# Cross-attention and mixture-of-experts kernel: value tiles, gate and ranks moved to the end of TensorE's turn

## Chip, cores and metric

The kernel runs on one core of a Trainium2 chip, in one launch. The metric is the device time of an execution in microseconds (us). A measured difference of about 0.3% is what can be told from none.

## The reference

One layer on x [16, 256, 512] with a context [16, 256, 256]. It is float32; the mask is all true.

```python
x = x + xattn(layernorm(x), ctx, mask, Wq, Wk, Wv, Wo)
x = x + ffn(layernorm(x), ...)
# xattn: 16 heads of 128, 8 key/value heads (two query heads share one)
scores = q @ k.T / sqrt(128); attn = softmax(scores); out = (attn @ v) @ Wo
# ffn: sigmoid gate over 32 experts, in 4 groups of 8; the 2 best groups, then the 4 best experts
# slot = how many earlier tokens (of all 4096) chose the same expert; those past CAP are dropped
h = silu(buf @ w1[e]) * (buf @ w3[e]); y = h @ w2[e]        # 32 experts, 512 -> 256 -> 512
out = sum_k weight_k * y_k + (silu(x @ sg) * (x @ su)) @ sd  # plus a shared expert, 512 wide
```

Since slots count tokens in order, the ranks (how many earlier tokens chose the same expert) are accumulated batch after batch.

## The kernel before

**Numbers.** Every float32 product is made from float16 halves: a value is split into a high half (`.hi`, written by ScalarE) and a low half (`.lo`, the rest, by VectorE or GpSimdE), and `products` issues three matmuls, high x high, high x low, low x high (lines 1777 to 1779). So each PSUM result that is used further is read twice: ScalarE's `..._high`, then VectorE's `..._low`.

**Turns.** The main part is a loop of 128 turns (`TURNS`), i = 8 b + j: batch b (16), key/value head j (8). Four compute engines and SyncE (SP, which issues most DMAs) each have their own program, written out by hand and in order; they meet only at semaphores. In turn i TensorE does:
- `scores(i)`: 12 matmuls of 256 columns, into ps_score0 and ps_score1
- `filler(fill(b, j))`: one extra job into the bank ps_fill1: a value tile (6 matmuls of 512 columns; four per batch, for the batch after, in turns 1, 3, 4, 6; in the first two batches in other turns), or in turn 5 the gate of the batch before (24 small ones)
- `query(i + 1)`: 24 matmuls of 256 columns; `key(i + 1)`: 6, into ps_fill1 as well
- `attend(i - 1)`: 6 matmuls of 512 columns, into ps_score1; its left operand are the probabilities turned by DMA
- `project(i - 2)`: 21 matmuls of 256 columns into ps_out0, ps_out1, ps_head and ps_fill0, where they add up over the 8 turns of a batch
- in turn 7 the ranks of the batch before (5 small ones), into ps_fill1.

The jobs that share ps_fill1 have one order, the list `held`; each waits (`emptied`) until the one before it has been read: keys by `key_low`, value tiles by `value_low` (VectorE, line 1352), the gate by `gate_exp_neg` (ScalarE), ranks by `place` (VectorE).

**The other engines in turn i.** VectorE: `maxima(i)` (line 1411, four, from ps_score), the batch's own work for that turn, the filler's `value_low`, `prob_scales` (lines 1418 and 1420, after ScalarE's exponentials), `query_low(i + 1)` (1346), two `probs_low` (1436), `key_low(i + 1)` (1341), `last_high` (1427), two more `probs_low`, then more of the batch's work. ScalarE: `sums_high(i - 2)` (1083), exponentials (1061) with the filler's `value_high` (984) between the second and the third, `query_high` (977), two `probs_high` (1069), `key_high` (971), the third, then `head_copy(i - 1)` (1076), which reads what attend wrote. GpSimdE: `sums_low(i - 2)` (786: one operation of 896 columns), the work of the batch, then `sums(i - 1)` (778, 779, 781), sums and differences of the copied head output. The projection is a product of 2 x 2 blocks with 7 products instead of 8, and these sums are its operands; `project` waits for `sum_lo`.

**Work of a batch, by turn j.** VectorE: turn 0 `place`, `pick(position)`, `find_slots` of b - 2, and at its end `pick(score)`, `choose_9` to `choose_11` (the weights); turn 1 at its end `residual_first`; turn 2 `residual_rest` (1308 to 1316), at its end the statistics of x1 (1263, 1268); turn 3 at its end the statistics of x of the next batch; turn 4 `xn2_rest` (1362); turn 5 `xn_rest` (1357), at its end `choose_0`, `choose_1`; turn 6 `choose_2` to `choose_4`, at its end `choose_5`, `choose_6`; turn 7 `choose_7`, `choose_8`, and `ctx_low`. GpSimdE: turn 3 `inv_std` of x1 (726, 729) and `x1_norm` (748, two tiles), turn 4 `inv_std` of x and `x_norm` (738, two tiles), turns 1, 2, 5, 6 a quarter each of `record` (831, indirect DMAs that write the table of slots). ScalarE and SP follow: `xn2_high` in turn 3, `xn_high` in turn 4, `turn_xn2` in turn 4, `turn_xn` in turn 6.

In the first batch the weights are split too (`weight_high`, `weight_low`, and `combine` on GpSimdE for Wo).

**After the loop.** The shared expert runs in `piece`s: up pieces (two products, tanh, product) and down pieces, which ScalarE copies to `shared_y`, from where `add_shared` adds them to the output by an accumulating DMA (815). ScalarE's copy of group n waits until the additions of group n - 2 have landed; those of groups 1 and 2 are counted together. Then come the 32 experts with gathered rows.

## Time and profile before

| | us |
|---|---|
| median of three runs | 1707.92 |
| lowest, highest | 1705.89, 1711.77 |
| profiled execution, its own time | 1704.77 |
| its span, first to last instruction | 1703.0 |
| matmuls busy | 1585.2 (93%) |
| VectorE busy | 1380.7 (81%) |
| ScalarE busy | 1053.2 (62%) |
| GpSimdE busy | 1035.9 (61%) |
| mean granted clock of TensorE | 0.987 |

PE is TensorE's matmul side, PEld its weight loads, DVE VectorE, ACT ScalarE, POOL GpSimdE. Matmuls are pipelined: one of 256 columns lasts 0.27 us and the next starts 0.11 us after it, so distances between starts count, not durations. A row of windows gives the stretch from:to, its length, the busy time and count of PE, PEld, DVE, ACT and POOL, the granted clock, the DMA engines' busy share and GB/s. A row `L1352 ... out<-in` names the line, the tile written and those read; "arena" is a tile that holds weights, values and probabilities, h_both the head output, weight_in[1] the halves of its sums. A clock of 1.00 is 2.4 GHz. The loop begins at 17.97 us; batch 10, whose turns are shown below, from 805.76 to 881.27.

### The profile page before, as it was taken

Reading aid. Unit: us, or ns where it says so; the run is one execution under the profiler, and the core shown is the slowest. Engines: PE = TensorE matmul, PEld = TensorE weight load, DVE = VectorE, ACT = ScalarE, POOL = GpSimd, SP = SyncE. Lnnn points to the kernel's source line nnn. Section 1 sums busy time; section 2 is a strip of 40 time slices with the busy share of each in tenths; the row PEclk is TensorE's granted clock in tenths of the full one; section 3 lists DMA queues with packets and bytes.
Section 4 is the critical chain, followed back from the end, with each engine's and each line's share of the span. In section 5 each row is a group of like instructions: output and inputs, shape, how many; then the busy total and the mean of one; then the engine's idle time right before and its main releaser. Section 6 shows DMA issues by size and latency. Waiting matters only on the chain. (4 is left out here: it accounts for less than half of the span.)

```text
span 1703.0 us, 36611 instructions
## 1 busy us (share of the span) xinstructions
PE 1585.2 (93%) x12583; PEld 1186.1 (70%) x12583; DVE 1380.7 (81%) x3723; ACT 1053.2 (62%) x2487; POOL 1035.9 (61%) x1004
## 2 busy tenths in 40 slices
PE   7778999999999999999999999999999899999995
PEld 4556767777777777777777777777776666666662
DVE  7788989998998989899988999898777156766763
ACT  5666676766666666666667666666644156666663
POOL 2766585857667586767768586776766533434332
PEclk9899999999999999999999999999999999999998
DMA  7545774636455454545555454544765558988843
GB/s 208 142 89 110 151 170 101 125 61 134 91 104 104 92 119 76 132 87 117 96 100 107 88 119 77 130 89 100 149 187 198 149 175 228 253 239 237 243 75 50
DMA packets 403751, 225.72 MB, mean 133 GB/s; under 512 B 348769, under 2 KB 360033, under 8 KB 403185
## 3 DMA queue, kind: packets, MB, share of 16 engines
q1 hardware_dynamic: 387104, 197.05, 48.5%
q0 software_dynamic: 15904, 25.29, 8.6%
q8 instruction: 103, 1.69, 0.4%
q10 hardware_dynamic: 560, 1.05, 0.2%
q14 instruction: 80, 0.65, 0.1%
HBM read 95.54 MB, written 44.47 MB: 82 GB/s over the span
## 5 line engine op out<-in xcount | busy, mean ns | idle before, releaser
L786 POOL TENSOR_TENSOR weight_in<-h_both,weight_in 128x896 f16<-128x896 f32 x128 | 244.0, 1907 | 97.5 <-ACT weight_in L1083 97.5
L1777 PE MATMUL ps_query<-xn_both,arena 128*128 128x256 f16 x1056 | 288.7, 273 | 1.0 <-DMA xn_both<-xn_half 1.0
L1778 PE MATMUL ps_query<-xn_both,arena 128*128 128x256 f16 x1056 | 288.6, 273 | 0.0
L1779 PE MATMUL ps_query<-xn_both,arena 128*128 128x256 f16 x1056 | 288.5, 273 | 0.0
L1083 ACT ACTIVATE weight_in<-h_both 128x896 f16<-128x896 f32 x128 | 121.6, 950 | 260.1 <-POOL h_both L781 256.2
L1436 DVE SCALAR_TENSOR_TENSOR arena<-arena,prob_scale 128x256 f16<-128x256 f32 x512 | 270.8, 569 | 0.6 <-ACT arena L1069 0.6
L1061 ACT ACTIVATE arena<-arena,neg_max 128x256 f32<-128x256 f32 x512 | 253.0, 495 | 25.4 <-DVE neg_max L1411 25.2
L778 POOL TENSOR_TENSOR h_both<-h_both 128x256 f32<-128x256 f32 x128 | 112.4, 878 | 194.8 <-ACT h_both L1076 194.6
L1069 ACT ACTIVATE arena<-arena,prob_scale 128x256 f16<-128x256 f32 x384 | 179.5, 499 | 71.8 <-DVE prob_scale L1420 69.9
L1411 DVE CUSTOM_DVE_ANT_0 arena<-ps_score,mask_add 128x256 f32<-128x256 f32 x512 | 185.6, 418 | 42.4 <-PE ps_score L1779 41.4
L831 POOL DMA_INDIRECT slot_table<-entry,slot_at x128 | 135.9, 1062 | 45.7 <-issue 31.1
L1777 PE MATMUL ps_out<-arena,weight_in 128*128 128x256 f16 x512 | 141.4, 276 | 13.4 <-POOL weight_in L786 13.4
L1777 PE MATMUL ps_score<-k_both,q_t 128*128 128x256 f16 x512 | 139.6, 273 | 8.6 <-issue 8.4
L1779 PE MATMUL ps_out<-arena,weight_in 128*128 128x256 f16 x512 | 141.4, 276 | 0.0
L1778 PE MATMUL ps_out<-arena,weight_in 128*128 128x256 f16 x512 | 141.4, 276 | 0.0
L1779 PE MATMUL ps_score<-k_both,q_t 128*128 128x256 f16 x512 | 139.7, 273 | 0.0
L1778 PE MATMUL ps_score<-k_both,q_t 128*128 128x256 f16 x512 | 139.7, 273 | 0.0
L1777 PE MATMUL ps_fill<-ctx_both,arena 128*128 128x256 f16 x256 | 69.8, 273 | 56.2 <-DVE arena L1352 54.4
L1777 PEld LDWEIGHTS ps_query<-xn_both,arena 128*128 128x128 f16 x1056 | 103.5, 98 | 20.5 <-DMA xn_both<-xn_half 1.5
L1553 DVE SCALAR_TENSOR_TENSOR arena<-arena 128x1024 f16<-128x1024 f32 x96 | 116.8, 1225 | 1.0 <-ACT arena L1095 1.0
L1778 PEld LDWEIGHTS ps_query<-xn_both,arena 128*128 128x128 f16 x1056 | 103.5, 98 | 18.9
L1779 PEld LDWEIGHTS ps_query<-xn_both,arena 128*128 128x128 f16 x1056 | 103.5, 98 | 12.3
(339 smaller groups left out, 4831.0 us busy)
## 6 DMA issues: line engine op xcount, KB each, us to landing
arena<-w SPq DMA_DIRECT2D x96, 512.0 KB, 6.1
out_rows_dram<-weight_in POOLq DMA_DIRECT2D x32, 256.0 KB, 4.7
x_in<-x SPq DMA_DIRECT2D x15, 512.0 KB, 4.9
out_rows_dram<-x SPq DMA_DIRECT2D x30, 256.0 KB, 4.7
xn_rows<-xn_half SPq DMA_DIRECT2D x15, 512.0 KB
x2t_kept<-xn_both SPq DMA_DIRECT2D x13, 512.0 KB, 3.0
ctx_in<-ctx_t SPq DMA_DIRECT2D x16, 256.0 KB, 3.5
arena<-arena SPq DMA_TRANSPOSE x256, 3.1
```

The lines of the kernel that those rows point to most:

```text
L778: pool.tensor_tensor(o_full[:, 4:6, :], o_full[:, 0:2, :], o_full[:, 2:4, :], ALU.add).then_inc(*own.up())
L786: pool.tensor_tensor(l_t.lo, o_full[:, :, :], l_t.hi, ALU.subtract).then_inc(sum_lo, 1)
L831: pool.indirect_dma_start(slot_table, bass.IndirectOffsetOnAxis(ap=slot_at[z % 2][:, t, k:k + 1], axis=0), entry[z % 2][:, t, k, :], None, ...
L1061: act.activation(probs[:, c, :], probs[:, c, :], ACT.Exp, bias=neg_max[:, c:c + 1], scale=-1.0, accum_out=prob_sum[:, c:c + 1]).then_inc(e ...
L1069: act.activation(p_rows[:, c, 0, :], probs[:, c, :], ACT.Copy, scale=prob_scale[:, c:c + 1]).then_inc(norm_hi, 1)
L1083: act.activation(l_t.hi, o_full[:, :, :], ACT.Copy, scale=1.0).then_inc(sum_hi, 1)
L1411: dve.tensor_tensor_reduce(out=probs[:, c, :], in0=ps_score[h][:, t * S:(t + 1) * S], in1=mask_add[b % 2][:, :], scale=-SCORE_SCALE, scala ...
L1436: dve.scalar_tensor_tensor(p_rows[:, c, 1, :], probs[:, c, :], prob_scale[:, c:c + 1], p_rows[:, c, 0, :], ALU.mult, ALU.subtract).then_in ...
L1553: dve.scalar_tensor_tensor(expert_w[e % HELD].lo[:, at], expert_in[e % AHEAD][:, at], W_S, expert_w[e % HELD].hi[:, at], ALU.mult, ALU.sub ...
L1777: pe.matmul(dst, a.hi, b.hi, start=start and n == 0, stop=False, skip_group_check=shared)
L1778: pe.matmul(dst, a.hi, b.lo, start=False, stop=False, skip_group_check=shared)
L1779: m = pe.matmul(dst, a.lo, b.hi, start=False, stop=stop and n == len(pairs) - 1, skip_group_check=shared)
```

## The change

The extra job in ps_fill1 moves behind `project` in TensorE's turn. It is emptied in the next turn: by ScalarE first thing, by VectorE after the maxima. The ranks of batch b - 2 become such a job, in turn 0 (place, pick(position) and find_slots in turn 1). `head_copy` moves ahead of ScalarE's third `probs_high`. `sums_low` becomes three operations of 256, 256 and 384 columns, and `sum_lo` counts three per turn. `x_norm` moves from GpSimdE to VectorE (turn 4), where `x_norm` was already defined for the first batch; `x1_norm` does one tile in turn 3 and one in turn 4. The high and low halves of xn2 and xn and their turning and storing move a turn later. Of the routing, `choose_0` and `choose_1` move from the end of turn 5 to that of 6, `choose_2` to `choose_4` from turn 6 to 7, `choose_5` and `choose_6` from the end of 6 to that of 7, `choose_7` and `choose_8` from 7 to the next turn 0, `pick(score)` to `choose_11` from the end of turn 0 to that of 3. After the loop, the second `add_shared` and two `late_split` come earlier in GpSimdE's order, and the pieces 0 and 1 and the last routing steps move.

```diff
@@ order of the jobs
+            if b > 1 and j == 0:
+                return ("rank", b - 2)
...
+            held += [("key", i + 1)] if i + 1 < TURNS else []
             held += [fill(b, j)] if fill(b, j) else []
-            held += [("key", i + 1)] if i + 1 < TURNS else []
-            held += [rank_of(b, j)] if rank_of(b, j) else []
+        held += [("rank", B - 2)]
@@ SP: turn_xn2 and store_xn2 from turn 4 to 5, keep_x2t from 6 to 7
-                if j == 4 and b:
+                if j == 5 and b:
                     for t in range(TB):
                         turn_xn2(b - 1, t)
@@ GpSimdE
             def sums_low(i):
                 pool.wait_ge(sum_hi, i + 1)
-                pool.tensor_tensor(l_t.lo, o_full[:, :, :], l_t.hi, ALU.subtract).then_inc(sum_lo, 1)
+                for at in (slice(0, 2), slice(2, 4), slice(4, LEFT)):
+                    pool.tensor_tensor(l_t.lo[:, at, :], o_full[:, at, :], l_t.hi[:, at, :], ALU.subtract).then_inc(sum_lo, 1)
...
-                if 1 <= i <= KV:
-                    combine(i - 1)
...
-                if j == 3 and b:
-                    x1_norm(z)
-                if j == 4 and a < B:
-                    x_norm(a)
-                if j in (1, 2, 5, 6) and b > 1:
-                    record(b - 2, (1, 2, 5, 6).index(j))
+                if j in (3, 4) and b:
+                    x1_norm(z, j - 3)
+                if j in (5, 6, 7) and b > 1:
+                    record(b - 2, j - 5)
+                if j == 0 and b > 2:
+                    record(b - 3, 3)
...
+                if i < KV:
+                    combine(i)
...
             add_shared(0)
+            add_shared(1)
             for part in range(RECORDS):
                 record(z, part)
...
-            add_shared(1)
+            for k in (20, 21):
+                late_split(k)
             pool.wait_ge(in_table, 16)
@@ ScalarE
+                if i:
+                    filler(fill(*divmod(i - 1, KV)))
                 if i >= 2:
                     sums_high(i - 2)
                 exps(i, range(0, TB))
...
-                filler(fill(b, j))
                 exps(i, range(TB, CELLS))
...
                 if i + 1 < TURNS:
                     key_high(i + 1)
-                probs_high(i, range(TB, CELLS - 1))
                 if i:
                     head_copy(i - 1)
-                if j == 3 and b:
+                probs_high(i, range(TB, CELLS - 1))
+                if j == 4 and b:
                     for t in range(TB):
                         xn2_high(b - 1, t)
-                if j == 4 and b + 1 < B:
+                if j == 5 and b + 1 < B:
                     for t in range(TB):
                         xn_high(b + 1, t)
@@ VectorE
                 maxima(i)
+                if i:
+                    filler(fill(*divmod(i - 1, KV)))
...
-                if j == 0 and b > 1:
+                if j == 1 and b > 1:
                     place(b - 2)
                     dve.wait_ge(placed, b - 1)
                     pick(position)
                     find_slots(b - 2)
                 if j == 2 and routed:
                     residual_rest(z)
-                if j == 4 and routed:
-                    for t in range(TB):
-                        xn2_rest(z, t)
-                if j == 5 and a < B:
+                if j == 4 and a < B:
+                    x_norm(a)
+                if j == 6 and a < B:
                     for t in range(TB):
                         xn_rest(a, t)
-                if j == 6 and routed:
+                if j == 7 and routed:
                     choose_2()
                     choose_3()
                     choose_4()
-                if j == 7 and routed:
+                if j == 0 and b > 1:
                     choose_7()
-                    choose_8(z)
-                filler(fill(b, j))
+                    choose_8(b - 2)
                 prob_scales(i)
...
@@ TensorE
                 scores(i)
-                filler(fill(b, j))
                 if i + 1 < TURNS:
                     for h in range(PAIR):
                         query(i + 1, h)
...
-                if i == TURNS - 1:
-                    piece(1)
                 if i >= 2:
                     project(i - 2)
-                filler(rank_of(b, j))
+                filler(fill(b, j))
```

## Rows read from the trace of the kernel before

**Rows 1.** Windows: one batch's turns 0, 2 to 7; twelve batches; two batches.
```profile
805.76:814.45 8.69, 8.45 (x75) 6.60 (x72) 8.45 (x24) 5.31 (x15) 4.11 (x4) 1.00 0.44 63
...
825.28:833.45 8.17, 8.17 (x71) 6.76 (x69) 7.83 (x22) 5.68 (x15) 5.28 (x7) 1.00 0.40 46
833.45:843.28 9.83, 9.63 (x77) 7.26 (x75) 8.65 (x26) 6.71 (x18) 9.21 (x9) 1.00 0.75 179
843.28:853.69 10.41, 9.63 (x78) 7.27 (x75) 9.08 (x24) 7.90 (x19) 10.16 (x10) 1.00 0.81 130
853.69:862.46 8.77, 8.77 (x95) 7.34 (x93) 7.71 (x19) 5.68 (x16) 6.30 (x7) 1.00 0.42 110
862.46:872.97 10.51, 9.63 (x77) 7.27 (x75) 10.04 (x44) 6.37 (x16) 6.44 (x7) 1.00 0.58 111
872.97:881.27 8.30, 8.30 (x76) 6.88 (x74) 7.17 (x21) 5.57 (x15) 3.85 (x5) 1.00 0.58 104
276.77:1183.32 906.55, 865.80 (x7266) 679.93 (x7264) 818.35 (x2438) 595.01 (x1548) 638.41 (x612) 1.00 0.50 102
...
117.93:276.77 158.84, 145.81 (x1218) 113.82 (x1216) 144.45 (x410) 108.04 (x275) 102.86 (x97) 1.00 0.65 137
```

**Rows 2.** Waits, 276.77 to 1183.32 us: who for whom, total, times, longest.
```profile
PE ps_fill L1777 <- DVE arena L1352: 36.2, 47, 1.2
```

**Rows 3.** Timeline of TensorE, turn 6: start, duration, instruction, [idle before].
```profile
863.77 0.38 PE L1777 MATMUL ps_fill<-arena,ctx_both 128*128 128x512 f16 x1
...
865.07 0.27 PE L1777 MATMUL ps_query<-xn_both,arena 128*128 128x256 f16 x1
...
867.58 0.27 PE L1779 MATMUL ps_query<-xn_both,arena 128*128 128x256 f16 x1
868.73 0.27 PE L1777 MATMUL ps_fill<-ctx_both,arena 128*128 128x256 f16 x1 [0.88 <-DVE arena L1352]
```

**Rows 4.** Timeline of VectorE, turns 2 and 3 of the batch.
```profile
826.69 0.41 DVE L1411 CUSTOM_DVE_ANT_0 arena<-ps_score,mask_add 128x256 f32<-128x256 f32 x1
...
828.06 0.69 DVE L1308 SCALAR_TENSOR_TENSOR x<-ps_out,x 128x512 f32<-128x512 f32 x1
...
830.71 0.17 DVE L1418 RECIPROCAL prob_inv<-prob_sum 128x4 f32<-128x4 f32 x1
...
832.85 0.34 DVE L1427 TENSOR_SCALAR arena<-arena,prob_scale 128x256 f16<-128x256 f32 x1
...
834.38 1.27 DVE L1263 BATCH_NORM_STATS2 stats<-x 128x6 f32<-128x512 f32 x2
...
835.85 0.41 DVE L1411 CUSTOM_DVE_ANT_0 arena<-ps_score,mask_add 128x256 f32<-128x256 f32 x1
...
839.12 0.18 DVE L1418 RECIPROCAL prob_inv<-prob_sum 128x4 f32<-128x4 f32 x1 [0.23 <-ACT arena L1061]
```

**Rows 5.** Timeline of VectorE, turns 0 and 1 of the batch.
```profile
815.79 0.74 DVE L1515 TENSOR_TENSOR picked<-one_hot,score 128x128 f32<-128x128 f32 x2
...
817.98 0.42 DVE L1411 CUSTOM_DVE_ANT_0 arena<-ps_score,mask_add 128x256 f32<-128x256 f32 x1
```

**Rows 6.** Timeline of GpSimdE, turns 3 and 4 of the batch.
```profile
843.09 0.73 POOL L778 TENSOR_TENSOR h_both<-h_both 128x256 f32<-128x256 f32 x1
...
846.09 2.00 POOL L786 TENSOR_TENSOR weight_in<-h_both,weight_in 128x896 f16<-128x896 f32 x1
```

**Rows 7.** The page's groups: busy time, mean ns, idle before.
```profile
L786 POOL TENSOR_TENSOR weight_in<-h_both,weight_in 128x896 f16<-128x896 f32 x128 | 244.0, 1907 | 97.5 <-ACT weight_in L1083 97.5
```

**Rows 8.** Timeline of VectorE, turn 4 of the batch.
```profile
845.66 2.98 DVE L1362 SCALAR_TENSOR_TENSOR xn_half<-weight_in,xn_half 128x512 f16<-128x512 f32 x2
```

**Rows 9.** One line's instructions on VectorE: shortest, median, longest ns.
```profile
L1284 DVE TENSOR_SCALAR x<-x_in,mean_var,rstd x2: 529/738/948, 6.5 to 7.4; 128x512 f32<-128x512 f32 x2
```

**Rows 10.** Timeline of ScalarE, turn 4 of the first batch.
```profile
81.28 0.63 ACT L991 ACTIVATE xn_half<-x 128x512 f16<-128x512 f32 x1 [1.44 <-POOL x L738]
```

**Rows 11.** Timeline of ScalarE after the last turn.
```profile
1340.93 0.60 ACT L1042 ACTIVATE weight_in<-ps_query 128x512 f32<-128x512 f32 x1 [10.35 <-DMA out_rows_dram<-weight_in]
```

More of the change, by code:

```diff
@@ L425, in fill @@
             return None
-        def rank_of(b, j):
-            return ("rank", b - 1) if j == KV - 1 and b else None
         before = {}
@@ L1054, in filler @@
                     value_high(ps_fill[1], *at)
-                else:
+                elif kind == "gate":
                     gate_exp_neg(*at)
@@ L1646, in dve_program @@
                     query_low(i + 1)
+                else:
+                    piece(0)
                 probs_low(i, range(0, TB))
@@ L1654, in dve_program @@
                     ctx_low(1)
-                if i == TURNS - 1:
-                    piece(0)
-                if j == 0 and b > 1:
-                    pick(score)
-                    choose_9()
-                    choose_10()
-                    choose_11(b - 2)
                 if j == 1 and routed:
@@ L1666, in dve_program @@
                         x1_stats_row(z, t)
+                if j == 3 and b > 1:
+                    pick(score)
+                    choose_9()
+                    choose_10()
+                    choose_11(b - 2)
                 if j == 3 and a < B:
@@ L1669, in dve_program @@
                         x_stats_row(a, t)
-                if j == 5 and routed:
+                if j == 4 and routed:
+                    for t in range(TB):
+                        xn2_rest(z, t)
+                if j == 6 and routed:
                     choose_0(z)
                     choose_1()
-                if j == 6 and routed:
+                if j == 7 and routed:
                     choose_5()
```

56 lines of the change are left out of this document (26 added, 30 removed).

## The prediction

> **What bounds the kernel now.** I read the windows of one steady batch first, turn by turn, then who waits for whom, then the timelines of TensorE, VectorE and GpSimdE around the waits. Batches 3 to 14 take 906.55 us together, 75.55 each, at full granted clock [rows 1]. A turn without extra work is 8.17 us of TensorE (turn 2 of a batch, no idle time); the gate matmuls add 0.60 (turn 5: 8.77), the ranks 0.13 (turn 7: 8.30) [rows 1], and a value tile 1.30 (its first matmul to the first of the query) [rows 3]. With four value tiles a batch is 8 x 8.17 + 4 x 1.30 + 0.60 + 0.13 = 71.3 us of TensorE. So 4.25 us per batch are waits: 0.5 in turn 0, 0.36 in turn 3, 0.94 in turn 4, 1.04 in turn 6, and by difference 1.4 in turn 1 [rows 1].
>
> Nearly all of it has one cause. The key matmuls write the PSUM bank that the value tile of the same turn has just filled, and VectorE's value_low empties that bank only behind the maxima: 47 waits, 36.2 us as the view counts idle time [rows 2]. In turn 6 the queries' last matmul starts 1.15 us before the key's first (867.58, 868.73), where 0.11 is the normal distance [rows 3]. TensorE is the bound, then, and VectorE holds it for about 1 us in the value turns. But VectorE is no idle helper: 818.35 of the 906.55 us are busy [rows 1].
>
> **The change, part by part.**
>
> *Value tile, gate, ranks at the end of the turn.* TensorE's work is the same. The tile is now read by ScalarE first thing in the next turn, during the scores, and by VectorE after its maxima; the next key comes 12 + 24 matmuls of 0.109 us (12 scores take 1.31 [rows 1, 3]) = 3.93 us after the turn's start. Maxima can start about 1.0 us in (an estimate: half of the scores, 0.65, and the 0.27 that a matmul takes [rows 3]); they take 1.37 (826.69 to 828.06) and value_low about 0.7, as other steps of its size from PSUM do [rows 4]. It ends at 3.1: the wait of 4.25 per batch goes wherever VectorE comes to its maxima on time, with 0.8 us to spare. Queued behind value_low is residual_rest in turn 2, x_norm in turn 4, choose_2 to 4 in turn 7, and then prob_scales, for which ScalarE waits.
>
> *Where VectorE is not on time.* The parts of VectorE per turn, by start-to-start times. Turn 2: maxima from 1.0 to 2.4, value_low to 3.1 (new here), residual_rest 2.65 (828.06 to 830.71) to 5.7, prob_scales up to the end of key_low 2.14 (830.71 to 832.85, where the next step starts) to 7.9. That is inside 8.17, by 0.3. The rest of the probabilities takes 1.53 (832.85 to 834.38), the statistics 1.47 (834.38 to 835.85) [rows 4]: VectorE ends at 10.9, which is 2.7 into turn 3. Before, it was 2.4 into it (835.85 against 833.45) [rows 1, 4].
> Turn 3: maxima start to reciprocal took 3.27 (835.85 to 839.12) with ScalarE's value copy in between [rows 4]; without its 0.6 (estimate from the 0.7 of its VectorE twin) 2.7. So reciprocal at 5.4, key_low done at 7.5, probabilities at 9.1, and 0.3 more because the head copy now stands before ScalarE's third probabilities: 9.4. Now the moved weights of the routing, pick(score) to choose_11: 2.19 (815.79 to 817.98) [rows 5], plus 0.5 for a collision (below): 12.1. The statistics of x, 1.47: 13.6. Turn 3 is 9.47 long, so VectorE is 4.1 into turn 4, less what turn 3 itself waits.
> Turn 3's own wait: GpSimdE's inv_std now as before waits for the statistics (2.7), takes about 1 us (in turn 4 the sums start at 843.09 with 0.73, 2.0 in all by estimate, and the low halves at 846.09 [rows 6]), and the low halves follow in 2.4: 6.2. TensorE's projection needs them at 8.17 - 21 x 0.109 = 5.88; before, the tile stood in between. Wait 0.35.
> Turn 4: maxima from 3.8 to 5.1, value_low to 5.9, key possible at 3.93: wait 1.95. Behind it x_norm (1.5), then probabilities; key_low ends before 9.6 and TensorE needs it at 8.17 + 1.95 = 10.1. Turn 5 has almost nothing for VectorE, and it catches up. Turns 6, 7, 0, 1 I find without a wait: the long steps end after 7 to 8 us against the 8.17.
> Waits after: 0.35 + 1.95 = 2.3 per batch instead of 4.25. Saving 1.95, twelve batches: **23.4 us**.
> Bounds: if VectorE loses no time to collisions and the weights overlap better, 1.3 are left (saving 35); if it loses another 2 us between turn 2 and turn 4, 4.3 are left (saving 0).
>
> *Three short low-half operations instead of one.* One operation of 896 columns is 1.9 us on average [rows 7] and 2.00 here; 256 columns take 0.73 [rows 6]. From these two the fixed part is about 0.25, so three cost 0.73 + 0.73 + 0.96 = 2.4: half a microsecond more on GpSimdE and later for the projection. In turn 4 the single operation ended 4.8 after the turn's start (848.09 against 843.28) with inv_std's 1.0 ahead of it; elsewhere that makes 3.8, with the half 4.3, against 5.88: a margin of 1.6. If each part also waits for one two-input step of VectorE of 0.69, three cost 4.5, and the margin is gone. What they give: VectorE's pair of xn2_rest took 2.98 us (845.66) where a step of this size takes 0.69 [rows 4, 8]; 1.7 were lost until GpSimdE's 2.00 us operation ended at 848.09 [rows 6]. With short ones a loss is at most about 1. The Trainium skill, "SBUF — State Buffer", section "Who interferes with whom", gives the rule: the read port that the two share is held for a whole instruction and the other engine blocks fully, when VectorE has two SBUF inputs or a two-port mode; the trace agrees here (1.7 us). By the same rule x_norm, moved to VectorE, can be blocked too, which speaks against that part; its two tiles would be 1.9 instead of 1.5 and the sum 0.4 per batch worse at most, and only if key_low were then late, which it is not.
>
> *x_norm from GpSimdE to VectorE, x1_norm in two turns.* VectorE takes 0.74 per tile, 0.53 to 0.95 [rows 9]: 1.5 in turn 4, behind value_low, hidden under the wait counted above; GpSimdE is rid of both tiles. Halving x1_norm lets the sums of turn 3 go first. The turned and stored xn rows move a turn later on SP, past one turn_probs, but queries need them only in the next batch's first turn; I cost them at nothing. Cover: about 4 us, and a miss would stand in turn 7.
>
> *Head copy sooner, routing later.* The copy comes when the attend matmuls end, so at most 0.5 us sooner: nothing by itself. The choose steps moved from turn 7 to 0 and the slots from 0 to 1 take the load from the turn that ran 8.45 busy of 8.69 [rows 1]; counted above. Records move with them, on a GpSimdE that has room.
>
> *Start and end.* In turn 4 of the first batch ScalarE waits twice some 1.5 us for GpSimdE's x_norm (81.28) and the weights of the next turns queue behind it [rows 10]. That goes, but the loads of wo bound the turns after it: **4 us**, between 0 and 8. Batches 1 and 2 take 158.84 for 72.6 + 71.3 of work, 15 us of waits [rows 1]; the same cause, one value tile more: **7 us**, between 3 and 11. At the end ScalarE waits 10.35 us for an accumulating DMA (1340.93) [rows 11]. The second such transfer is issued sooner, but ScalarE waits for the third as well, and that one stays behind the gathers with two more splits ahead of it: no gain there; about **1 us** from earlier attention in the last turn.
>
> **Sum.** 23.4 + 4 + 7 + 1 = 35 us. The profiled execution took 1704.77 (span 1703.0), so 1669.5; the median of the runs shown is 3.15 above it: 1672.5, said as 1672.
>
> **Rivals.**
> 1. *No waits left.* VectorE is on time everywhere, as in turn 6: 12 x 4.25 = 51, start 8, batches 1 and 2 11, end 1: 71 us, 1637. Against it: turns 2 to 4 carry 2.19 more than before in turn 3 and 0.7 more in turn 2.
> 2. *The wait only moves.* The key waits for value_low as long in turn 4 as in all turns now: 0 from the steady batches and 8 to 12 from the rest: 1697. For it: every microsecond of lateness between turn 2 and turn 4 is a microsecond of TensorE, twelve times, and GpSimdE now puts six blocking operations where there were four.
> 3. *Slower: the projection waits for the low halves in every turn.* It comes 1.3 us sooner in four turns, its operand 0.5 to 2.6 later. If the three parts end 0.8 after TensorE is ready, that is 8 x 0.8 = 6.4 per batch against 4.25, and 12 x 2.15 = 26 us: 1734. It decides from 0.53 us per turn. Against it: the margin of 1.6.
>
> **How the numbers follow.** My forecast 0.62 (own range 1656 to 1688), rival 1 0.13, rival 2 0.16, rival 3 0.07, something else slower 0.02. A measurement of this kernel tells about 0.3% (5 us) from no change. Rival 2 gives half of its chance to a gain over that and half to none; so faster 0.83, same 0.08, slower 0.09. The range takes in rival 2 and most of the way to rival 1: 1648 to 1697.
>
> **What would show it.** TensorE's waits on ps_fill from L1352's successor gone in turns 1, 3 and 6, and left in turn 4, near 2 us; steady batches near 73.6 us; VectorE's maxima of turn 4 3 to 4 us after the scores' start; three GpSimdE operations of 0.7 to 1.0 us; no DVE pair near 3 us. I am wrong if ps_out waits for GpSimdE in several turns of a batch, if a batch is under 72 us, or if the key waits in turns 1, 3 or 6.

## The result and the profile after

The changed kernel takes 1712.39 us (median of 20 runs, 1706.55 to 1716.11), the kernel before, run beside it, 1707.81. The ratio is 1.0023, 95% interval 1.0014 to 1.0032: slower by 0.23%, some 4 us, where 35 us were forecast as a gain. The profiled executions took 1711.89 and 1704.77 us, with spans of 1710.2 and 1703.0.

The windows of a usual steady batch (number 13, turns 0 to 7), turn 4 of batch 10, then batches 3 to 14, batches 1 and 2 and the first batch. After the length stand the busy times (and counts) of TensorE's matmuls and weight loads, VectorE, ScalarE and GpSimdE, the granted clock, the DMA share and GB/s.

```profile
1037.47:1046.12 8.65, 8.46 (x76) 6.79 (x74) 8.34 (x29) 5.57 (x15) 6.35 (x8) 1.00 0.47 121
1046.12:1056.06 9.94, 9.64 (x82) 7.19 (x80) 9.57 (x27) 5.46 (x15) 5.66 (x9) 1.00 0.42 79
1056.06:1064.54 8.48, 8.33 (x70) 6.67 (x69) 8.34 (x23) 6.12 (x16) 2.84 (x6) 1.00 0.21 41
1064.54:1074.53 9.99, 9.80 (x75) 7.17 (x76) 8.76 (x25) 5.71 (x16) 8.77 (x12) 1.00 0.69 175
1074.53:1086.15 11.62, 9.63 (x77) 7.28 (x76) 11.29 (x33) 7.18 (x18) 7.60 (x10) 1.00 0.46 65
1086.15:1095.12 8.97, 8.94 (x94) 7.27 (x93) 8.07 (x21) 7.31 (x18) 6.74 (x10) 1.00 0.75 120
1095.12:1104.59 9.47, 9.47 (x83) 7.33 (x79) 8.36 (x22) 5.80 (x16) 7.71 (x9) 1.00 0.84 181
1104.59:1112.76 8.17, 8.17 (x71) 6.75 (x70) 7.86 (x34) 6.26 (x16) 5.66 (x8) 1.00 0.19 36
...
847.46:860.75 13.29, 11.30 (x76) 7.96 (x75) 12.96 (x35) 7.18 (x18) 8.38 (x10) 0.87 0.44 70
...
282.36:1187.56 905.20, 870.89 (x7263) 679.77 (x7260) 844.81 (x2461) 592.37 (x1548) 617.44 (x780) 1.00 0.51 102
126.75:282.36 155.61, 147.09 (x1213) 114.12 (x1212) 143.74 (x401) 108.48 (x275) 97.70 (x122) 0.99 0.62 135
17.74:126.75 109.01, 79.03 (x540) 56.81 (x541) 82.57 (x174) 66.48 (x148) 58.75 (x72) 0.87 0.49 128
```

A steady batch takes 75.43 us (905.20 / 12), before 75.55 [rows 1]; 73.6 was forecast. Turns 6 and 7 have no wait left, and turn 4 waits 11.62 - 9.47 = 2.15, close to the forecast 1.95. Against the forecast turn by turn the excess is 0.35, 0.47, 0.31, 0.17, 0.20, 0.20, 0 and 0, or 1.7 per batch. The average of the twelve is 0.14 above this batch. In two of them, 3 and 10, turn 4 takes 13.3 us: the granted clock is 0.87 there, because it fell to half (the 1.2 GHz level) for 3.4 us, within 1.4 us of the end of the key's wait of 1.99. The matmuls are busy 11.30 instead of 9.63, so this costs 1.7 us each time, 0.28 per batch on average; in the other ten, eight of them with the same wait, the clock stayed at 1.00.

By stretches the 7.2 us of span are: first batch 99.96 to 109.01 (+9.05, forecast -4), batches 1 and 2 -3.23 (forecast -7), steady batches -1.35 (forecast -23.4), turns 0 to 7 of the last batch up to the last scores +0.86, the end +2.10 (forecast for both together -1), and -0.23 ahead of the first turn. These are one profiled execution of each kernel, and a few microseconds of such a difference are its scatter (see below the table).

The largest waits of TensorE's matmuls in batches 3 to 14 of the changed kernel (who for whom, total, times, longest):

```profile
PE ps_fill L1776 <- DVE arena L1346: 22.7, 12, 2.0
PE ps_score L1776 <- DMA arena<-arena: 7.2, 14, 1.5
PE ps_score L1776 <- DVE neg_max L1405: 1.3, 7, 0.2
```

The key's wait for value_low was met 47 times before [rows 2]; it is met 12 times now, once per batch, in turn 4. The two rows of ps_score are the heads' matmuls (attend): 8.5 us. They are not quite new: in the kernel before they waited twice, 1.0 us in all. They write the bank that the scores filled, so they wait for the maxima of their own turn, and they read the turned probabilities of the turn before. The forecast followed the key, the projection and the scores, and never these. By the distances between the matmuls' starts they now wait 0.29, 0.44 and 0.36 us in turns 0, 1 and 3; the 0.2 in turn 5 stands before the key, as in turn 4. TensorE's timeline in turns 0, 1 and 4 of batch 13 (start, duration, instruction, [idle before]):

```profile
1042.41 0.38 PE L1776 MATMUL ps_score<-arena 128*128 128x512 f16 x1 [0.19 <-DVE neg_max L1405]
...
1051.18 0.38 PE L1776 MATMUL ps_score<-arena 128*128 128x512 f16 x1 [0.30 <-DMA arena<-arena]
...
1080.61 0.27 PE L1776 MATMUL ps_fill<-ctx_both,arena 128*128 128x256 f16 x1 [1.99 <-DVE arena L1346]
```

And VectorE from turn 3 into turn 4:

```profile
1067.56 0.41 DVE L1405 CUSTOM_DVE_ANT_0 arena<-ps_score,mask_add 128x256 f32<-128x256 f32 x1
...
1074.48 1.01 DVE L1509 TENSOR_TENSOR picked<-one_hot,score 128x128 f32<-128x128 f32 x2
...
1076.79 0.17 DVE L1530 TENSOR_TENSOR entry<-weight,weight_inv 128x8 f32<-128x8 f32 x1
1076.87 1.28 DVE L1257 BATCH_NORM_STATS2 stats<-x_in 128x6 f32<-128x512 f32 x2
...
1078.35 0.41 DVE L1405 CUSTOM_DVE_ANT_0 arena<-ps_score,mask_add 128x256 f32<-128x256 f32 x1
...
1079.72 0.75 DVE L1346 SCALAR_TENSOR_TENSOR arena<-ps_fill,value_scale,arena 128x512 f16<-128x512 f32 x1
```

The maxima of turn 4 start 3.82 us into the turn (1078.35 - 1074.53; forecast 3.8), behind weights of 2.39 (1076.87 - 1074.48) and statistics of 1.5. So the mechanism of turn 4 is as forecast. What was not forecast shows in the groups of VectorE over the twelve batches, the low halves and the last high half of the probabilities, before and after (mean ns behind the busy time):

```profile
L1436 DVE SCALAR_TENSOR_TENSOR arena<-arena,prob_scale 128x256 f16<-128x256 f32 x386 | 197.3, 552 | 0.0
L1427 DVE TENSOR_SCALAR arena<-arena,prob_scale 128x256 f16<-128x256 f32 x96 | 35.3, 368 | 0.0
```
```profile
L1430 DVE SCALAR_TENSOR_TENSOR arena<-arena,prob_scale 128x256 f16<-128x256 f32 x385 | 234.6, 649 | 4.8 <-issue 3.1 <-ACT arena L1062 0.8
L1421 DVE TENSOR_SCALAR arena<-arena,prob_scale 128x256 f16<-128x256 f32 x96 | 44.6, 465 | 0.0
```

The same instructions take longer: (234.6 - 197.3 + 44.6 - 35.3) / 12 = 3.9 us more of VectorE per batch in these two groups.

### The profile page after: what moved, and what is told of

The parts are those of the page before. It is cut to its first block and busy times, and to the rows that moved or that the text cites. A ratio compares the mean times of both kernels' runs of the same rounds, so it can differ in the third digit from the quotient of the medians.

```text
span 1710.2 us, 36852 instructions
## 1 busy us (share of the span) xinstructions
PE 1593.9 (93%) x12583; PEld 1187.5 (69%) x12583; DVE 1411.9 (83%) x3753; ACT 1050.2 (61%) x2487; POOL 1010.9 (59%) x1230
## 5 line engine op out<-in xcount | busy, mean ns | idle before, releaser
L778 POOL TENSOR_TENSOR weight_in<-h_both,weight_in 128x256 f16<-128x256 f32 (+1 forms) x384 | 299.4, 807 | 123.8 <-ACT weight_in L1076 114.7
L1430 DVE SCALAR_TENSOR_TENSOR arena<-arena,prob_scale 128x256 f16<-128x256 f32 x512 | 312.4, 650 | 18.7 <-ACT arena L1062 14.5
L769 POOL TENSOR_TENSOR h_both<-h_both 128x256 f32<-128x256 f32 x128 | 101.5, 793 | 139.8 <-ACT h_both L1069 139.5
L1776 PE MATMUL ps_score<-arena 128*128 128x512 f16 x256 | 98.1, 383 | 16.4 <-DMA arena<-arena 11.0
L1777 PEld LDWEIGHTS ps_query<-xn_both,arena 128*128 128x128 f16 x1056 | 103.5, 98 | 12.2
L1778 PEld LDWEIGHTS ps_query<-xn_both,arena 128*128 128x128 f16 x1056 | 103.5, 98 | 12.1
```

Source lines behind the costliest of these rows:

```text
L769: pool.tensor_tensor(o_full[:, 4:6, :], o_full[:, 0:2, :], o_full[:, 2:4, :], ALU.add).then_inc(*own.up())
L778: pool.tensor_tensor(l_t.lo[:, at, :], o_full[:, at, :], l_t.hi[:, at, :], ALU.subtract).then_inc(sum_lo, 1)
L1430: dve.scalar_tensor_tensor(p_rows[:, c, 1, :], probs[:, c, :], prob_scale[:, c:c + 1], p_rows[:, c, 0, :], ALU.mult, ALU.subtract).then_in ...
L1776: pe.matmul(dst, a.hi, b.hi, start=start and n == 0, stop=False, skip_group_check=shared)
L1777: pe.matmul(dst, a.hi, b.lo, start=False, stop=False, skip_group_check=shared)
L1778: m = pe.matmul(dst, a.lo, b.hi, start=False, stop=stop and n == len(pairs) - 1, skip_group_check=shared)
```

## The experiments

In this table all spans are of profiles. "Steady" is batches 3 to 14 divided by 12; "end" is from the last turn's scores to the end. "Profiled" is the time of the execution that the spans are from. Stretches come from the starts of the scores' first matmuls; the ratio is to the kernel before, run beside it.

```
kernel                          median   ratio (95%)              profiled  first   steady  end
before                          1707.8                           1704.8    99.96   75.55  458.6
after                           1712.4   1.0023 (1.0014-1.0032)  1711.9   109.01   75.43  460.7
late_head                       1687.7   0.9882 (0.9865-0.9899)  1689.1   104.20   74.19  462.7
early_head                      1757.3   1.0290 (1.0271-1.0308)  1750.7   105.19   78.00  457.4
one_low                         1719.7   1.0075 (1.0056-1.0094)  1712.2   107.27   75.43  461.5
tiles_alone                     1706.5   0.9995 (0.9983-1.0006)  1704.3   101.89   75.15  457.2
fill_move                       1681.8   0.9849 (0.9828-0.9870)  1679.0   101.15   74.00  456.7
copy_soon_sums_wait             1695.4   0.9925 (0.9905-0.9945)  1695.4   109.19   74.12  462.0
one_low_late_head               1682.0   0.9845 (0.9825-0.9865)  1683.6   105.88   73.80  460.8
norm_end_late_head              1678.4   0.9822 (0.9803-0.9840)  1676.4   102.06   73.43  462.6
sums_after_lows                 1693.9   0.9912 (0.9898-0.9926)  1695.1   106.07   74.36  462.4
weights_t5                      1680.6   0.9835 (0.9819-0.9851)  1680.8   111.41   72.81  464.0
weights_t5_late_head            1666.7   0.9760 (0.9740-0.9780)  1666.4   104.17   72.55  463.0
w5_late_head_norm_end           1664.6   0.9741 (0.9725-0.9757)  1665.4   103.27   72.53  463.0
w5_late_head_one_low_norm_end   1669.0   0.9774 (0.9760-0.9789)  1668.6    98.86   73.09  463.5
fill_move_w5                    1716.6   1.0052 (1.0038-1.0066)  1713.4   101.23   75.90  464.1
slots_after_residual            1691.3   0.9900 (0.9885-0.9914)  1691.3   105.56   74.18  464.4
```

Kernels whose first batch is the same program show how far single profiles scatter: 109.01 (after) and 111.41 (weights_t5); 104.20, 104.17 and 105.56 (late_head, weights_t5_late_head, slots_after_residual); 102.06 and 103.27 (the two with x_norm behind the probabilities and three low halves). The clock's share of it shows in the granted clock of the first batch, 0.86 to 0.92 in these.

### The place of the head copy

late_head undoes it in the changed kernel:

```
-                if i:
-                    head_copy(i - 1)
                 probs_high(i, range(TB, CELLS - 1))
+                if i:
+                    head_copy(i - 1)
```

> The changed kernel with one part undone: ScalarE copies the heads after its third probabilities again, as before the change. Theory (start): in turn 2 of the first batch the sooner copy waits for GpSimdE's low halves behind a weight combination, ScalarE's third probabilities wait behind it, the load of x queues behind the turned probabilities and the next weights behind that; so the first batch falls from 109.0 us back to about 100, steady batches stay at 75.4, and the time is about 1703, ratio to the kernel before 0.997. Rival (the place of the copy costs nothing, the first batch is late because of the tiles or because the combinations stand elsewhere): within 1.5 us of the changed kernel, 1712.

early_head makes the opposite edit in the kernel before.

> The kernel before with one part of the change alone: the head copy in front of ScalarE's third probabilities. Theory (start): the first batch gets 5 to 9 us longer (99.96 us before), the rest stays, so 1713 to 1717, ratio 1.003 to 1.005. Rival (costs nothing): ratio within 0.001 of 1.

1687.7, 24.7 us under the changed kernel and far more than the 9 expected: the first batch gives 4.8, batches 1 and 2 give 2.9, and a steady batch 1.24 (14.9 in all), which the theory had called unchanged. Of these 1.24, 0.28 are the two falls of the clock, which late_head doesn't have in batches 3 to 14. By the matmuls' starts the heads' waits fall from 1.1 to 0.5 per batch, and the key's in turn 4 from 2.05 to 1.64.

In the kernel before, the edit costs 50 us where 5 to 9 were expected, 2.45 in each steady batch. Some 1.4 of the 2.45 are clock: in ten of the twelve batches the granted clock of turn 1 is 0.87 or 0.88, and the turn takes 13.3 to 14.1 us, where it takes 11.8 and 12.1 in the two others and 10.8 in the kernel before. In each of the ten the clock fell after a wait of 2.0 to 2.8 us. By the trace the wait comes from VectorE, which is late because its low halves wait for ScalarE's third probabilities, 37.7 us in the twelve steady batches. Turn 1 of batch 10, and that group:

```profile
845.63:859.53 13.90, 11.30 (x77) 7.79 (x75) 10.41 (x28) 6.33 (x16) 7.06 (x10) 0.88 0.28 54
```
```profile
L1436 DVE SCALAR_TENSOR_TENSOR arena<-arena,prob_scale 128x256 f16<-128x256 f32 x384 | 211.7, 591 | 39.9 <-ACT arena L1069 37.7
```

In the changed kernel that wait is small (0.8). What the copy does there can be read in turn 2. Changed kernel, ScalarE, GpSimdE and VectorE:

```profile
1063.70 0.59 ACT L1069 ACTIVATE h_both<-ps_score 128x512 f32<-128x512 f32 x1
1064.18 0.50 ACT L1062 ACTIVATE arena<-arena,prob_scale 128x256 f16<-128x256 f32 x1
```
```profile
1064.37 0.91 POOL L769 TENSOR_TENSOR h_both<-h_both 128x256 f32<-128x256 f32 x1 [3.84 <-ACT h_both L1069]
1065.24 0.64 POOL L770 TENSOR_TENSOR h_both<-h_both 128x128 f32<-128x128 f32 x1
```
```profile
1064.72 1.45 DVE L1430 SCALAR_TENSOR_TENSOR arena<-arena,prob_scale 128x256 f16<-128x256 f32 x2
```

late_head, GpSimdE and VectorE in the same turn of batch 10:

```profile
820.29 0.91 POOL L769 TENSOR_TENSOR h_both<-h_both 128x256 f32<-128x256 f32 x1 [3.50 <-ACT h_both L1069]
```
```profile
820.14 1.34 DVE L1430 SCALAR_TENSOR_TENSOR arena<-arena,prob_scale 128x256 f16<-128x256 f32 x2
```

With the sooner copy GpSimdE's sums have begun when VectorE comes to its pair of low halves, and both halves of the pair meet them (0.85 and 0.68 us one by one); with the late copy the first half starts ahead of the sums (0.48 and 0.95). In this turn that is only 0.1 us. Over the twelve batches the low halves fall from 649 to 614 ns on average, and the last high half, which meets the sums in turns 0, 1 and 7, from 465 to 354:

```profile
L1430 DVE SCALAR_TENSOR_TENSOR arena<-arena,prob_scale 128x256 f16<-128x256 f32 x386 | 221.5, 614 | 0.0
L1421 DVE TENSOR_SCALAR arena<-arena,prob_scale 128x256 f16<-128x256 f32 x96 | 34.0, 354 | 0.0
```

Together that is 2.0 us of VectorE per batch, and its maxima of turn 4 start 3.3 us into the turn instead of 3.7. The next run tells that from ScalarE's order. It keeps the copy where the change has it and holds the sums back until the third probabilities are made:

```
                 pool.wait_ge(head_copied, i + 1)
+                if i + 1 < TURNS:
+                    pool.wait_ge(norm_hi, (CELLS - 1) * (i + 2))
```

> The changed kernel, head copy where it has it, with one more wait: GpSimdE's sums of the heads start only when ScalarE has made the third probabilities of the turn, which is when they start in late_head. Theory (steady batches: not ScalarE's order costs, but the sums that start 0.5 us sooner and stand in the way of VectorE's low half of the third probabilities, 0.85 instead of 0.48 us): steady batches 74.2 plus or minus 0.3 as in late_head; the first batch stays at 109, since there ScalarE's probabilities themselves wait behind the copy; time 1694 to 1700. Rival (ScalarE's third probabilities 0.5 us later are the cost): steady batches 75.4, time 1710 to 1715.

As the theory had it: steady batches 74.12 as in late_head, first batch 109.19 as in the changed kernel, 1695.4. The low halves and the last high half are back at 621 and 359 ns. So in the steady batches it is the start of GpSimdE's sums, in the first batch ScalarE's order. The first batch, changed kernel, turn 2: GpSimdE's low halves stand behind a combination, the copy waits for them, the third probabilities for the copy, and on SP x and the next weights stand behind the turned probabilities (columns: start, duration).

```profile
48.09 2.16 POOL L778 TENSOR_TENSOR weight_in<-h_both,weight_in 128x256 f16<-128x256 f32 x3
```
```profile
50.34 0.60 ACT L1069 ACTIVATE h_both<-ps_score 128x512 f32<-128x512 f32 x1 [5.98 <-POOL weight_in L778]
50.83 0.50 ACT L1062 ACTIVATE arena<-arena,prob_scale 128x256 f16<-128x256 f32 x1
```
```profile
44.87 9.02 SPq L600 DMA_TRANSPOSE arena<-arena  x2
53.93 0.58 SPq L515 DMA_DIRECT2D x_in<-x  x1
54.55 0.48 SPq L500 DMA_DIRECT2D weight_in<-wq  x1
```

In the kernel before ScalarE made the third probabilities at 44.53, and SP issued these loads at 49.51 and 50.14:

```profile
44.53 0.50 ACT L1069 ACTIVATE arena<-arena,prob_scale 128x256 f16<-128x256 f32 x1
```
```profile
49.51 0.58 SPq L515 DMA_DIRECT2D x_in<-x  x1
50.14 0.48 SPq L500 DMA_DIRECT2D weight_in<-wq  x1
```

If VectorE pays for meeting the sums, can they be kept away altogether? sums_after_lows is late_head with the sums waiting for all four low halves (norm_lo).

> late_head with GpSimdE's sums of the heads held back until VectorE has made all low halves of the turn's probabilities. Theory (VectorE pays 0.47 us per turn for the sums that meet its last low half, 0.95 against 0.48): L1430 falls to about 0.5 us on average and steady batches to 73.5 or less, time 1676 to 1683. Rival (the sums are then 0.9 us later, and where VectorE is late, in turns 2 to 4, the projection waits for the low halves): 74.5 or more, 1690 or more.

```profile
L1432 DVE SCALAR_TENSOR_TENSOR arena<-arena,prob_scale 128x256 f16<-128x256 f32 x385 | 167.9, 477 | 0.0
```
```profile
PE ps_out L1778 <- POOL weight_in L780: 4.4, 8, 0.8
```

The mean falls to 477 ns, which is also what the two low halves in front of the sums take in late_head (475 to 479 on average in turns 0 to 6). VectorE is busy 737.5 us in the twelve batches where it was 824.2 in late_head. Yet a batch takes 74.36: the rival was right (it said 74.5 or more). The projection now waits for the low halves, in turn 0 of batch 10 by 0.69. The sums have to start early for the projection and late for VectorE, and the late copy lies between.

### Parts of the change alone

tiles_alone moves only the value tiles to the end of the turn, fill_move tiles and gate, both in the kernel before. The core of fill_move:

```
-                filler(fill(b, j))                 # TensorE, behind scores(i)
...
+                filler(fill(b, j))                 # TensorE, behind project(i - 2)
...
+                if i:                              # VectorE behind maxima(i), ScalarE first
+                    filler(fill(*divmod(i - 1, KV)))
```

> The kernel before with the value tiles alone moved to the end of TensorE's turn and read in the next; gate, ranks, routing, norms, head copy and low halves stay as before. Theory A (the tiles' move is good and the weights of the routing in turn 3 spoil it): no wait of the key in turns 3, 4 and 6, because VectorE reaches turn 4's maxima about 2 us sooner than in the changed kernel; steady batches 72 to 73 us, time 1665 to 1680. Theory B (what the tile at the start of the turn gave was time for the turned probabilities: without it the attention's matmuls wait for them in every value turn): the waits only change their place, batches 75 us or more, time 1703 to 1712.

> The kernel before with the first part of the change alone: value tiles and gate at the end of TensorE's turn, read first thing in the next; all of routing, norms, head copy and low halves as before. In tiles_alone the gate stood right behind the scores and waited 1.89 us per batch for VectorE to empty the value tile of the turn before; here that goes. Theory A (the gate's wait was the price): steady batches 73.0 to 73.6 us, time 1675 to 1686. Theory B (the waits only change their place; x_norm on GpSimdE makes the projection of turn 4 late by 1.0 as in tiles_alone, and VectorE's late turns do the rest): 74.5 or more, time over 1694.

tiles_alone is no faster than before (0.9995). Neither theory named the reason in advance: the gate, left behind the scores, waits for the tile of the turn before to be emptied.

```profile
858.12 0.19 PE L1788 MATMUL ps_fill<-gate_s,xn_both 128*128 128x32 f16 x1 [1.71 <-DVE arena L1362]
```

With the gate moved too this wait goes, and the move alone brings 1.5%, 1681.8 as expected, with steady batches of 74.00 (73.0 to 73.6 expected). The whole change, of which it is the first part, ends 31 us above it. one_low and one_low_late_head make GpSimdE's low halves one operation again:

```
-                for at in (slice(0, 2), slice(2, 4), slice(4, LEFT)):
-                    pool.tensor_tensor(l_t.lo[:, at, :], o_full[:, at, :], l_t.hi[:, at, :], ALU.subtract).then_inc(sum_lo, 1)
+                pool.tensor_tensor(l_t.lo, o_full[:, :, :], l_t.hi, ALU.subtract).then_inc(sum_lo, 1)
```

> The changed kernel with GpSimdE's low halves as one operation again. Theory of the prediction: the one operation is 0.3 to 0.5 us shorter than the three, so the projection's wait of 0.26 in turn 3 goes, but VectorE is blocked up to 1.7 us at a time again; steady batches 75.4 plus or minus 0.4, time 1707 to 1717. Rival (the three operations are what delays the projection and the heads everywhere): a batch 1 us shorter or more, 1700 or less.

> late_head with GpSimdE's low halves as one operation. Theory (three short operations give little here, they only share out the blocking): steady batches 74.2 plus or minus 0.4, time 1683 to 1693. Rival (they are needed: one_low was 7 us over the changed kernel in time): 1694 or more.

On the changed kernel one_low is slower, 1719.7 against 1712.4 (1707 to 1717 expected). Its profile can't show where, because the profiled execution was the fastest of its six, 1712.2, no slower than that of the changed kernel. Its steady batches are 75.43 as there, but without the two falls of the clock that hold 0.28 of the changed kernel's 75.43. On late_head one operation is faster (1682.0 against 1687.7, steady 73.80 against 74.19; 1683 to 1693 expected), and with the weights and x_norm moved it is slower again (1669.0 against 1664.6, steady 73.09 against 72.53, below). The three operations have no sign of their own; it depends on the kernel around them, and how was not shown.

### The weights of the routing

In the change they stand at the end of turn 3. This edit puts them into turn 5, with the records one turn on:

```
-                if j == 3 and b > 1:
+                if j == 5 and b > 1:
                     pick(score)
                     choose_9()
                     choose_10()
                     choose_11(b - 2)
```

> late_head (1687.7) with the weights of the routing (pick of the scores to choose_11, some 2.2 us of VectorE) moved on from the end of turn 3 to the end of turn 5, and the records one turn on. Theory (VectorE's load between turn 2 and turn 4 makes the key of turn 4 wait, 1.53 us in late_head): that wait goes and the 0.25 behind it in turn 5; steady batches 72.4 to 73.0 against 74.19, time 1670 to 1676. Rival (what VectorE does behind value_low, not when it comes to its maxima, is what TensorE waits for, or the load only moves to turn 6): 1685 or more.

> The changed kernel (1712.4, steady batches 75.43) with the weights of the routing in turn 5 and nothing else, the head copy where the change has it. Theory (the two causes are nearly independent; turn 4's wait of 2.15 and the second wait behind it are those of the weights): steady batches 72.9 to 73.7, time 1684 to 1692. Rival (the sooner copy makes VectorE late enough for the wait to stand in another turn): 1697 or more.

In both kernels the wait of turn 4 goes. Alone it brings 1680.6, 31.8 us under the changed kernel and more than expected; with the late head copy 1666.7, also more than expected. Windows of weights_t5 (the twelve batches; turn 4 of batch 10):

```profile
281.85:1155.57 873.72, 864.78 (x7263) 679.31 (x7260) 824.11 (x2462) 590.43 (x1548) 609.20 (x781) 1.00 0.53 106
827.15:836.76 9.61, 9.61 (x77) 7.25 (x76) 9.49 (x26) 7.30 (x18) 7.99 (x10) 1.00 0.48 88
```

Turn 4 is 9.61 where it was 11.62. The two edits overlap: the head copy is worth 1.24 per batch with the weights in turn 3 and 0.26 with them in turn 5; in time it is worth 24.7 and 13.9. The same edit on fill_move, where the weights stand in turn 0:

> fill_move (1681.8, steady batches 74.00) with the weights of the routing moved from the end of turn 0 to turn 5 and the records behind them; ranks, places and slots stay. Theory (the 2.2 us of weights make VectorE late in turn 1, where the attention waits 0.5 and the scores 0.4): these go, steady batches 73.2 to 73.5, time 1671 to 1677. Rival (turn 1 is late because of the slots in turn 0, the weights only fill up idle time): 1680 or more.

It went the other way, 1716.6. Turn 1 did get shorter (9.94 to 9.64 on average), but in turn 5 of fill_move_w5 VectorE still has choose_0 and choose_1 behind them, its maxima of turn 6 come 5.4 us into the turn (batch 10), and the heads' matmuls wait 2.3 us for them. Turn 6 is 11.8 to 12.2 in nine batches, and 13.4 to 14.5 in three where the granted clock of the turn is 0.87 or 0.88: 12.35 on average instead of 9.61. Steady batches make 23 of the 35 us, the end 7. One and the same move is worth -32 or +35 us; it depends on what stands behind it.

### x_norm, and the best of the parts

norm_end_late_head puts VectorE's x_norm of turn 4 behind its probabilities, on late_head; the other two add the weights in turn 5, one of them with a single low half.

```
-                if j == 4 and a < B:      # behind value_low, ahead of prob_scales
-                    x_norm(a)
...
+                if j == 4 and a < B:      # behind probs_low
+                    x_norm(a)
```

> late_head (1687.7, first batch 104.20 us) with VectorE's x_norm of turn 4 behind its probabilities instead of ahead of prob_scales. Theory (start: in turn 4 of the first batch x_norm waits 0.87 us for GpSimdE and takes 1.8, the turned probabilities and behind them on SP the next weights are that much later): the first batch falls by 1.5 to 3 us, steady batches 74.2 plus or minus 0.3; time 1684 to 1687. Rival (the first batch is bound by GpSimdE's combinations ahead of the low halves): no change in the first batch.

> The three edits that helped most, together: head copy late, weights of the routing in turn 5, x_norm behind the probabilities; three low halves. If they add up: 1687.7 - 21.0 - 9.4 = 1657, steady batches 71.8 to 72.1 us against 71.3 of work. If x_norm's gain in the steady batches (0.76 each in norm_end_late_head) came from the same lateness as the weights': 1660 to 1666.

> weights_t5_late_head (1666.7) with the low halves as one operation (which gave 5.7 us on late_head) and x_norm behind the probabilities. If the parts add up: 1659 to 1662; if the single low half and the weights in turn 5 aim at the same wait: 1664 to 1668.

The first batch falls by 2.1, inside the expected 1.5 to 3 but not far outside the scatter; that a steady batch falls by 0.76 too was not expected, and the time of 1678.4 is below the forecast 1684 to 1687. With the weights gone from turn 3 hardly any of it is left (72.55 to 72.53), so its gain was not one of its own; that it came from the same lateness of VectorE is the reading that the expectation had named (1660 to 1666 in that case, 1657 if the parts added up). w5_late_head_norm_end has the lowest time, 1664.6, ratio 0.9741: 2.6% under the kernel before. Its interval overlaps that of weights_t5_late_head (0.9760), so these two can't be told apart. With one low half it is 1669.0, above both values expected (1662 and 1668 at most).

### The end

On late_head, after the loop:

```
+            piece(3)
+            residual_first(z)
+            residual_rest(z)
+            for t in range(TB):
+                x1_stats_row(z, t)
             place(z - 1)
...
             choose_11(z - 1)
-            piece(3)
-            residual_first(z)
...
-            for part in range(RECORDS // 2):      # GpSimdE
-                record(z - 1, part)
             inv_std(1, z, x1_stats, x1_rstd, x1_normed)
+            for part in range(RECORDS // 2):
+                record(z - 1, part)
```

> late_head (1687.7; from the last turn's scores to the end 462.65 us, against 458.63 in the kernel before and 456.69 in fill_move), with the slots and weights of batch 14 behind the residual of the last batch on VectorE after the loop, and two records of GpSimdE behind the last inv_std. Theory (routing later leaves 4 us of slots and weights and four records of 1 us each between the last projection and the normalisation of the last batch, and TensorE waits 2.2 and 2.3 us for pieces queued behind): the end gets 2 to 4 us shorter, 459 to 461, time 1683.5 to 1686. Rival (the end is bound elsewhere, by the adds of the shared groups): the waits there only move, end 462 or more, time within 1 us of late_head.

The theory fell: the end doesn't get shorter (464.4 against 462.7), and neither does the time (1691.3 against 1687.7, intervals that overlap). TensorE now waits in one piece where it waited in two:

```profile
1260.93 0.39 PE L1776 MATMUL ps_query<-arena,ctx_both 128*128 128x512 f16 x1 [4.80 <-DVE hidden L1371]
```

fill_move's end takes 456.7, so what the end costs comes from the rest of the change; which part was not found.

## Why the prediction was wrong

**Turn by turn.** Right: the key's wait goes in turns 1, 3 and 6 and stays in turn 4; its size (1.95, measured 2.15), its cause (VectorE 3.8 into the turn) and what causes that (weights_t5). Luck has a part in the size: with the head copy late VectorE comes 3.3 us into the turn and the key waits 1.64 on average (3.7 and 2.05 with the copy soon), so the 0.5 that the sum held for a collision and the 0.3 for ScalarE's order stood in for a cost that was elsewhere put at nothing. The three low halves take 2.4 us (807 ns each on average), as forecast. None of the three signs of being wrong showed (a batch under 72 us, the key waiting in turns 1, 3 or 6, the projection waiting in several turns): none of them looked at the heads' matmuls.

**The failed step: "Head copy sooner ... at most 0.5 us sooner: nothing by itself".** It is worth 24.7 us of the 40 by which the result missed the forecast; the share depends on what stands around it, 13.9 with the weights in turn 5. The half microsecond was about right: the sums start 0.45 us sooner after the heads' matmuls on average, 0.8 in turn 0. But it was priced only by who waits for the copy, not by what the copy releases (GpSimdE's sums, on top of VectorE's last high and low halves; 14.9 us in the steady batches, 3.4 of them clock) and not by what is queued behind it on ScalarE (the third probabilities; in the first batch 4.8 us). The prediction knew the interference [rows 4, 6, 8], had a number for it, and applied it to the operations that were cut or moved, not to those whose start moved. The Trainium skill, "SBUF — State Buffer", section "Who interferes with whom", says that the ports which VectorE and GpSimdE share are an exclusive lock, and that the order of issue decides who is blocked. The runs agree: the low half takes 477 ns when the sums are kept away and 649 on average in the changed kernel, and a shift of the sums' start by 0.5 us changes which half waits and for how long.

**"Turns 6, 7, 0, 1 I find without a wait."** True for 6 and 7. Turns 0 and 1, and turn 3 too, wait 0.3 to 0.45 on average in the heads' matmuls, whose needs the working left out: 1.1 us per batch. The tile at the start of a turn had also been 1.3 us in which maxima and turned probabilities could be late; fill_move, where it alone has gone from there with the gate, has such waits in turns 0, 1 and 3 as well (0.2, 0.5 and 0.3).

**The start, "4 us".** +9.05. Of the 13 between, the head copy is 4.8, x_norm ahead of prob_scales 2.1 more. x_norm did leave GpSimdE, and the key's wait of turn 5 fell from 6.8 to 1.1 in late_head, but the projection of that turn waits 5.3 instead: by that trace the load of wo is issued at 82.45, behind the turned probabilities, GpSimdE waits for it to land, combines from 86.66 to 91.10, makes the low halves up to 93.64, and the projection starts at 93.70. The rest, some 6, was not taken apart by runs. By the profiles of the changed kernel and the one before, the projection's waits for GpSimdE's low halves rise from 12.2 to 24.8 us in the first batch, the key's for value_low fall from 7.3 to 0.4, and the matmuls are busy 3.6 longer (79.03 against 75.48), at a granted clock of 0.87 against 0.90: a part of the 9.05 is clock.

**Batches 1 and 2, "7 us".** 3.23, and 6.1 with the late head copy: right but for that.

**The end, "1 us".** +3.0 together with the last batch. That routing later costs there was argued from the trace and refuted by slots_after_residual; open.

**The rivals.** Nearest was rival 2, the waits only move, with 0.16, and no gain in the steady batches (0.12 each). But of the 4.1 us that a batch still waits only 2.15 stand in turn 4, 1.1 are at the heads' matmuls, and with the start's loss its 1697 was still too low. Rival 3 (the projection waits for the low halves in every turn) did not happen; the range ended 15 us under the result.

## What to carry to other kernels

An instruction moved half a microsecond forward also moves forward all that it releases: look at what the released work meets, not only at who was waiting. Before an edit is costed at nothing, list every instruction of the bounding engine with all its waits; one left out (here the heads' matmuls) is where the slack goes. And a change of many parts is worth running by parts: here one part alone gave 1.5%, and the whole with two of its parts put elsewhere 2.4%, where the whole as it was gave nothing. Last, look at the granted clock of a stretch before its time is put down to a wait: here waits of 2 us and more were followed in some turns, and in others not, by matmuls that took 1.7 us more.

## What the runs showed of the hardware

Keeping GpSimdE's sums off VectorE's low halves (steps with two inputs in SBUF) cuts those from 614 to 477 ns on average, and VectorE is busy 87 us less in twelve batches (824.2 to 737.5; 54 of it in these steps). The kernel is not faster for it (74.36 us per batch against 74.19): busy time freed on the engine that looks fullest was worth nothing there. From the changed kernel to late_head VectorE is busy only 1.7 us less per batch (844.8 to 824.2), the projection doesn't wait longer for the sums (0.05 us per batch in turn 3 against 0.19), and a batch is 1.24 us shorter, 0.28 of it clock.

Not every operation of GpSimdE is in the way. In the changed kernel 44 of the low halves run wholly inside a GpSimdE tensor_scalar (the normalisation, 2.1 us, one tensor input), and they take 474 to 481 ns; in the kernel before it is 89, with 471 to 486. Those of the changed kernel that overlap one of GpSimdE's tensor_tensor operations (two tensor inputs) take 797 ns on average, up to 1336.

The granted clock fell to half for 3.4 us in ten of early_head's twelve steady turns 1, each time after a wait of 2.0 to 2.8 us, and cost 1.7 us of matmuls. In the two other batches it stayed at 1.00 behind waits of 2.2 and 2.4. After the wait of 1.99 in turn 4 of the changed kernel it fell in two batches, and in eight with the same wait it did not. What decides was not found.
